# A two-layer transformer on one core: rows of scales loaded behind x, q's ones filled on GpSimd, 26 warm-up products, and the first turned maxima behind all parts

## The chip, the cores and the metric

The kernel runs on one core of a Trainium2 chip. The metric is the device time of one execution in microseconds; the median of several executions is compared. The core has five engines with a queue of instructions each: TensorE (PE, products), VectorE (DVE), ScalarE (ACT), GpSimd (POOL) and SyncE (SP, which here only issues transfers). They meet at semaphores only.

## The reference

x (1024 tokens of 256 numbers) passes through two layers; each adds attention and then a feed-forward block, both of the normalised x:

```
x = x + attn0(layernorm(x))     # 16 heads of 16; q, k, v, o with biases; ALiBi; causal
x = x + ffn0(layernorm(x))      # silu(gate) * up, then down; weights are int32 less 128, times a scale per row
x = x + attn1(layernorm(x))     # as above without biases and ALiBi
x = x + ffn1(layernorm(x))      # weights rounded to float8 e4m3, times a scale per column
```

ALiBi adds `slope[h] * (key - 1023)` to each score. A softmax needs the largest score of each query; the kernel computes it in full.

## The kernel before

**Exact products from bf16 parts.** q and k come from products in float32 (`qk` jobs 0 to 7: first q and k of heads 0 to 7 for tokens 0 to 511, jobs 0 and 1, then of heads 8 to 15, jobs 2 and 3, then the same for tokens 512 to 1023, jobs 4 to 7). Each result is split into three bf16 parts (high on ScalarE, middle on ScalarE, low on VectorE), and SyncE copies them by transfers inside the core's memory, six for each job, into `qS` and `kS`, where 96 rows (16 numbers of a head, six times) make one contraction. Below these 96 rows stand in the first layer three rows of ALiBi (in `kS`: the bias in three bf16 parts; in `qS`: ones) and two rows for the negated maximum of the query (in `kS`: ones; in `qS`: the maximum in two parts). So the score that goes into the exponential has its maximum taken off already.

**Attention** runs over 8 groups of 4 heads and 512 queries (`CGS`), in an order written out beforehand (`attention_order`): scores for the maxima (`max_scores`, L668 to L676) that VectorE reduces (L1091), a turn of a group's maxima (`turn`, L739; VectorE copies them to `mT`, L1104; SyncE sends them to `qS`, L440, `spread_max`), the scores again with the maximum taken off (`exp_scores`, L690), the exponential on ScalarE (L982), a cut along the diagonal on GpSimd (L521) and the product with v (L710). Ahead of the first exp step stand 21 score products of the first two groups and the first turn; between them TensorE does side jobs (v, the turning of the first feed-forward's weights and of the second layer's). The first exp product of a group waits for its `mT` transfer, and everything behind it on TensorE's queue waits with it. At most three score products are ahead of VectorE (three banks).

**The start.** SyncE loads x in three pieces, Wv and Wo, the tails of `kS` and `qS` (ALiBi rows and ones), then the rows of scales (`col_rows`, eight small transfers, L416 to L421) and the bias bo; ScalarE's queue loads bq, bk, Wq and Wk. TensorE runs `WARM` products of no use (L833), turns the normalised x (L616), and computes jobs 0 to 3 (L848); the second half of x is turned between jobs 1 and 2. ScalarE first puts Wq in the order by dimension (`turn_w0(0)`, L918), copies the four turned tiles out (L887), does the same for Wk and then the parts of the jobs (L910 high, L894 middle). Ahead of job 4, `turn_cols` (L828) turns the rows of scales into columns: TensorE waits there for all eight transfers, and behind it for Wv and Wo. The first feed-forward's weights are converted on GpSimd with these scales (L545).

**SyncE's order** behind the loads is a loop over the eight jobs (`spread`, L434), with the loads of other weights ahead of jobs 2 and 4, and the first group's maxima at `FIRST_MAX_BEFORE`, ahead of job 6:

```
for k in range(N_QK):
    ...
    if k == FIRST_MAX_BEFORE:
        spread_max(L, 0)
    spread(L, k)
for cg in range(1, N_CG):
    spread_max(L, cg)
```

Of the kernel before, what the change touches and what calls it, by code (L numbers as in the profile page):

```python
# [26 lines left out]
P = 128  # L27
T, C = 1024, 256
NH, HD = 16, 16
HID0, HID1 = 704, 768  # L30
NT = T // P
CH = 512
# [14 lines left out]
N_COLS = COL_S1 + 2 * HT  # L47
ZERO_POINT = 128.0
SCALE = float(HD) ** -0.5

F32, BF16, FP16, I32 = mybir.dt.float32, mybir.dt.bfloat16, mybir.dt.float16, mybir.dt.int32
ALU = mybir.AluOpType
# [6 lines left out]
QK_ROWS = len(Q_PARTS) * HD  # L59

ALIBI_ROWS = (3, 0)
MAX_ROWS = 2
X_PIECES = (slice(0, 2), slice(2, TPC), slice(TPC, NT))
TAIL_GAP = 32
K_MAX = [QK_ROWS + a for a in ALIBI_ROWS]
K_EXP = [k + MAX_ROWS for k in K_MAX]


def qk_job(n):

    return n // 2 % CJ, n // (2 * CJ), n % 2


N_QK = CJ * NC * 2
# [69 lines left out]
TURN_AHEAD = 5  # L144
FIRST_HALF_AFTER = 5
QK_FIRST = 2
WARM = 60
COLS_BEFORE = 4
V_FIRST = (5, 2)
FIRST_TURN_AHEAD = 7  # L150
FFN0_AFTER = 2
W1_AFTER = 4
FIRST_MAX_BEFORE = 6
PV_LAG = 1
W8_DOWN_AT = 3

# [82 lines left out]
def alibi_tail():  # L239

    bf16 = mybir.dt.np(BF16)
    start = 2.0 ** -0.5
    slopes = np.array([start * start ** i for i in range(NH)], np.float32)
    bias = slopes[:, None] * (np.arange(T, dtype=np.float32) - np.float32(T - 1))[None, :]
    rest = bias.astype(np.float32) / np.float32(SCALE)
    rows = []
    for _ in range(3):
        part = rest.astype(bf16)
        rows.append(part)
        rest = rest - part.astype(np.float32)  # L250
    rows += [np.ones((NH, T), bf16)] * (MAX_ROWS + ALIBI_ROWS[0])
    apart = np.zeros((len(rows), NH * NC, CH + TAIL_GAP), bf16)
    apart[:, :, 0:CH] = np.stack(rows).reshape(len(rows), NH * NC, CH)
    return apart


def two_layer_kernel(nc, a, out, tail):
    with ExitStack() as ctx:
        def sb(name, shape, dt):
            return ctx.enter_context(nc.sbuf_tensor(name, shape, dt))  # L260

        def sem(name):
            return ctx.enter_context(nc.semaphore(name))
# [11 lines left out]
        v1 = sb("v1", [P, NT, NH, 2 * HD], F32)  # L275
# [8 lines left out]
        w0 = sb("w0", [P, 4, CJ, C], F32)  # L284
# [47 lines left out]
        mask_q = sb("mask_q", [P, P], BF16)  # L332
        mask_k = sb("mask_k", [P, P], BF16)
        q_flat = qS[:, :, :, :].rearrange("p c h t -> p (c h t)")
        q_chunks = q_flat.rearrange("p (n t) -> p n t", t=CH)
        k_chunks = kS[:, :, :].rearrange("p h t -> p (h t)").rearrange("p (n t) -> p n t", t=CH)
        fT = q_flat.bitcast(F32)[:, 0:HT * T].rearrange("p (k t) -> p k t", k=HT)

# [9 lines left out]
        w0_in, wvo_in = [sem(f"w0_in{m}") for m in range(2)], sem("wvo_in")  # L348
# [7 lines left out]
        tail_in = sem("tail_in")  # L356
# [2 lines left out]
        s_full, s_free = sem("s_full"), sem("s_free")  # L359
        m_full, m_free = sem("m_full"), sem("m_free")  # L360
        tri_done = sem("tri_done")
        ones_v = sem("ones_v")
        pv_done, o_taken = sem("pv_done"), sem("o_taken")
        consts, consts_step = sem("consts"), sem("consts_step")
        stats_done, rstd_done, xn_done = sem("stats_done"), sem("rstd_done"), sem("xn_done")
# [37 lines left out]
        @block.sync  # L403
        def _(sp):
            xin = a["L0_attn_x"].rearrange("o (t p) c -> p (o t) c", p=P)
            for piece, tiles in zip(x_in, X_PIECES):
                sp.dma_start(x[:, tiles, :], xin[:, tiles, :]).then_inc(piece, 16)
            for m, n in ((2, "Wv"), (3, "Wo")):
                sp.dma_start(w0[:, m], a[f"L0_attn_{n}"].rearrange("(j p) o -> p j o", p=P)).then_inc(wvo_in, 16)
            full = HID0 // P  # L410
            sp.dma_start(k_chunks[QK_ROWS:K_EXP[0]], tail[0:ALIBI_ROWS[0] + MAX_ROWS, :, 0:CH]).then_inc(tail_in, 16)
            sp.dma_start(q_chunks[QK_ROWS:K_MAX[0]], tail[ALIBI_ROWS[0] + MAX_ROWS:, :, 0:CH]).then_inc(tail_in, 16)
            sp.wait_ge(rows_zero, 1)
            for m, n in enumerate(("gate", "up")):
                s, row = a[f"L0_ffn_s_{n}"], COL_S0 + m * HT
                sp.dma_start(col_rows[row:row + full], s[0:full * P].rearrange("(k p) -> k p", p=P)).then_inc(rows_in, 16)  # L416
                sp.dma_start(col_rows[row + full:row + HT, 0:HID0 - full * P], s[full * P:HID0].unsqueeze(0)).then_inc(rows_in, 16)
            for row, n in ((COL_SD0, "L0_ffn_s_down"), (COL_BV, "L0_attn_bv"),
                           (COL_S1, "L1_ffn_gate_scale"), (COL_S1 + HT, "L1_ffn_up_scale")):
                whole = a[n].rearrange("(k p) -> k p", p=P)  # L420
                sp.dma_start(col_rows[row:row + whole.shape[0]], whole).then_inc(rows_in, 16)  # L421
            sp.dma_start(bo[:], a["L0_attn_bo"].unsqueeze(0).to_broadcast([P, C])).then_inc(bo_in, 16)

            def spread(L, k):

                mt, c, w = qk_job(k)
                heads = slice(mt * NH // CJ, (mt + 1) * NH // CJ)
                for part, done in enumerate((hi_done, mid_done, lo_done)):
                    sp.wait_ge(done, L * N_QK + k + 1)
                    for r, stands in enumerate((Q_PARTS, K_PARTS)[w]):  # L430
                        if stands == part:
                            rows = slice(r, QK_ROWS, len(Q_PARTS))
                            dst = qS[rows, c, heads, :] if w == 0 else kS[rows, heads, c * CH:(c + 1) * CH]
                            sp.dma_start(dst, part_slots[k][:, part]).then_inc(stacked[k], 16)  # L434

            def spread_max(L, cg):

                g, c = CGS[cg]
                sp.wait_ge(mT_done, L * N_CG + cg + 1)
                sp.dma_start(qS[K_MAX[L]:K_EXP[L], c, g * G:(g + 1) * G, :], mT[:, cg % 2, :]).then_inc(m_stacked[cg % 2], 16)  # L440

            for L in range(LAYERS):
                for k in range(N_QK):
                    if (L, k) == (0, FFN0_AFTER):
                        for m, n in enumerate(("gate", "up")):
                            w = a[f"L0_ffn_wq_{n}"]
                            sp.dma_start(g0[:, m, 0:full].bitcast(I32), w[0:full * P].rearrange("(k p) i -> p k i", p=P)).then_inc(ffn0_in, 16)
                            sp.dma_start(g0[0:HID0 - full * P, m, full].bitcast(I32), w[full * P:HID0]).then_inc(ffn0_in, 16)
                    if (L, k) == (0, W1_AFTER):
                        sp.dma_start(d0[:, :, :].bitcast(I32), a["L0_ffn_wq_down"].rearrange("(j p) i -> p j i", p=P)).then_inc(ffn0d_in, 16)  # L450
                        for m, n in enumerate(("Wq", "Wk", "Wv", "Wo")):
                            sp.dma_start(w1r[:, m], a[f"L1_attn_{n}"].rearrange("(j p) i -> p j i", p=P)).then_inc(w1_in, 16)
                    if k == FIRST_MAX_BEFORE:
                        spread_max(L, 0)
                    spread(L, k)
                for cg in range(1, N_CG):
                    spread_max(L, cg)
                if L == 0:
                    sp.wait_ge(pv_done, N_STEP)
                    sp.dma_start(k_chunks[K_MAX[1]:K_EXP[1]], tail[ALIBI_ROWS[0]:ALIBI_ROWS[0] + MAX_ROWS, :, 0:CH]).then_inc(ones_k, 16)  # L460
            yout = out.rearrange("o (t p) c -> p (o t) c", p=P)
            for t in range(NT):
                sp.wait_ge(x_final, t + 1)
                sp.dma_start(yout[:, t, :], x[:, t, :]).then_inc(stored, 16)
            sp.wait_ge(stored, 16 * NT)
# [3 lines left out]
        def _(pool):  # L469
            k = [0]  # L470
# [11 lines left out]
            for m in (ident, identb):  # L482
# [3 lines left out]
                                    pattern=[[-1, P]], channel_multiplier=1)  # L486
            nc.gpsimd.affine_select(out=mask_k[:], in_=mask_k[:], compare_op=ALU.is_ge, fill=NEG, base=0,
                                    pattern=[[1, P]], channel_multiplier=-1).then_inc(consts, 1)

            nc.gpsimd.memset(v1[:, :, :, HD:2 * HD], 1.0).then_inc(ones_v, 1)  # L490

            def round_columns(w, top, dst, cols):

# [39 lines left out]
            rstd_of(0)  # L533
            rstd_of(1)
            pool.wait_ge(rstd_done, 4)

            pool.wait_ge(ffn0_in, 16 * 4)
            pool.wait_ge(a_free, A_AT[("cols",)] + 1)
# [52 lines left out]
        def _(pe):  # L591
# [228 lines left out]
            def turn_bqk():  # L820
                bank = take_a(("bqk_cols",))
                pe.wait_ge(bqk_turned, 1)
                nc.tensor.transpose(bank[:, 0:2 * CJ], bqk_dims, ident[0:2 * CJ, 0:2 * CJ]).then_inc(a_full, 1)
# [7 lines left out]
            turn_bqk()  # L831
            for _n in range(WARM):
                nc.tensor.matmul(ps[:, 7, 0:P], identb[:], mask_q[:], start=True, stop=True)  # L833
            for L in range(LAYERS):
# [26 lines left out]
                    side_job(L, side)  # L861
                if L == 0:
                    pe.wait_ge(ones_v, 1)
                    pe.wait_ge(tail_in, 16 * 2)
                else:
                    pe.wait_ge(ones_k, 16)
                attention(L)
# [5 lines left out]
        def _(act):  # L873
# [52 lines left out]
            for L in range(LAYERS):  # L926
# [44 lines left out]
                for s in range(N_STEP):  # L971
# [7 lines left out]
                    for pair in range(G // 2):  # L979
                        m = 2 * n + pair  # L980
                        act.wait_ge(s_full, m + 1)
                        nc.scalar.activation(prob[:, n % 3, 2 * pair:2 * pair + 2, off:CH],  # L982
                                             ps[:, 2 * (m % 2):2 * (m % 2) + 2, off:CH], ACT.Exp, scale=SCALE).then_inc(s_free, 1)
                    if s >= PV_LAG:
# [275 lines left out]
```

## Time and profile before

| | us |
|---|---|
| median of three runs | 449.64 |
| the three runs | 448.88, 452.99, 449.64 |
| the profiled execution | 453.61 |
| its span, first to last instruction | 451.9 |

| engine | busy us | share of the span |
|---|---|---|
| TensorE | 419.5 | 93% |
| VectorE | 301.8 | 67% |
| ScalarE | 235.9 | 52% |
| GpSimd | 161.0 | 36% |

The mean granted clock of TensorE was 0.984 of full. Busy shares are means over stages that have different limits; the change touches only the first 70 us, so those are read by themselves. Times in the rows below are microseconds from the start of the span.

### The profile page before, as it was taken

Reading aid. Unit: us, or ns where it says so; the run is one execution under the profiler, and the core shown is the slowest. Engines: PE = TensorE matmul, PEld = TensorE weight load, DVE = VectorE, ACT = ScalarE, POOL = GpSimd, SP = SyncE. Lnnn points to the kernel's source line nnn. Section 1 sums busy time; section 2 is a strip of 40 time slices with the busy share of each in tenths; the row PEclk is TensorE's granted clock in tenths of the full one; section 3 lists DMA queues with packets and bytes.
Section 4 is the critical chain, followed back from the end, with each engine's and each line's share of the span. In section 5 each row is a group of like instructions: output and inputs, shape, how many; then the busy total and the mean of one; then the engine's idle time right before and its main releaser. Section 6 shows DMA issues by size and latency. Waiting matters only on the chain.

```text
span 451.9 us, 14543 instructions
## 1 busy us (share of the span) xinstructions
PE 419.5 (93%) x6326; PEld 237.9 (53%) x6326; DVE 301.8 (67%) x609; ACT 235.9 (52%) x383; POOL 161.0 (36%) x242
## 2 busy tenths in 40 slices
PE   5799989999999979999999998998999999798997
PEld 5356654455555347434467455644545553374476
DVE  4635699999996129322234577999999971197883
ACT  3534546677687862211100552455776778724950
POOL 4108323202202222295961000235362463220780
PEclk9979999999999999999999999999999999998999
DMA  7899450000000000202000468500000000000002
GB/s 201 136 246 268 95 141 4 4 3 4 4 3 5 3 7 0 71 1 70 1 0 0 109 181 209 137 4 4 3 4 4 4 5 2 2 1 0 2 23 71
DMA packets 21657, 22.97 MB, mean 51 GB/s; under 512 B 2588, under 2 KB 20858, under 8 KB 21594
## 3 DMA queue, kind: packets, MB, share of 16 engines
q1 hardware_dynamic: 20498, 19.03, 17.4%
q0 software_dynamic: 544, 2.49, 1.9%
q8 instruction: 50, 0.82, 0.8%
q10 hardware_dynamic: 552, 0.53, 0.4%
q14 instruction: 13, 0.11, 0.1%
HBM read 8.27 MB, written 1.05 MB: 21 GB/s over the span
## 4 chain that ended last, share of the span: by engine, by line
PE 69%; DVE 17%; ACT 5%; DMA 3%; issue 2%; SPq 2%; POOL 1%; ACTq 0%; DVEq 0%
DVE mx L1091 11%; PE ps L710 10%; PE ps L690 10%; PE ps L668 10%; PE ps L793 9%; PE ps L808 5%; PE ps L848 5%; PE ps L798 5%; ACT prob L982 4%; PE ps L607 4%; PE ps L816 3%; DMA col_rows<-in_L_ffn_up_scale 3%; PE ps L676 1%; DVE stats L1055 1%; DVE xn L1164 1%
## 5 line engine op out<-in xcount | busy, mean ns | idle before, releaser
L1091 DVE TENSOR_REDUCE mx<-ps 128x1 f32<-128x512 f32 (+3 forms) x304 | 182.2, 656 | 24.5 <-PE ps L676 21.9
L982 ACT ACTIVATE prob<-ps 128x1024 f32<-128x1024 f32 (+1 forms) x192 | 145.5, 812 | 70.1 <-PE ps L690 69.5
L668 PE MATMUL ps<-kS,qS 99*32 99x512 bf16 (+21 forms) x1536 | 113.7, 320 | 4.8 <-DVE mx L1091 2.9
L521 POOL TENSOR_SCALAR_AFFINE_SELECT prob<-prob 128x256 f32<-128x256 f32 x128 | 51.9, 412 | 159.5 <-ACT prob L982 158.2
L690 PE MATMUL ps<-qS,kS 101*32 101x512 bf16 (+7 forms) x1536 | 96.3, 327 | 3.8 <-ACT prob L982 3.5
L710 PE MATMUL ps<-prob,v 128*32 128x512 f32 (+3 forms) x768 | 80.2, 489 | 2.1 <-POOL prob L521 1.4
L668 PEld LDWEIGHTS ps<-kS,qS 99*32 99x32 bf16 (+1 forms) x1536 | 43.5, 95 | 53.5 <-DVE mx L1091 30.1
L690 PEld LDWEIGHTS ps<-qS,kS 101*32 101x32 bf16 (+1 forms) x1536 | 35.4, 96 | 32.5 <-ACT prob L982 16.8
L673 PE MATMUL ps<-mask_q,identb 128*32 128x32 bf16 (+1 forms) x1024 | 51.6, 185 | 0.0
L676 PE MATMUL ps<-mask_q,identb 128*32 128x96 bf16 (+1 forms) x512 | 45.9, 197 | 0.0
L793 PE MATMUL ps<-xnT,gu0T 128*128 128x512 f32 (+1 forms) x96 | 42.2, 596 | 0.7 <-ACT xnT L887 0.7
L673 PEld LDWEIGHTS ps<-mask_q,identb 128*32 128x32 bf16 x1024 | 28.5, 97 | 10.9 <-issue 6.2
L676 PEld LDWEIGHTS ps<-mask_q,identb 128*32 128x32 bf16 x512 | 28.8, 98 | 5.4
L793 PEld LDWEIGHTS ps<-xnT,gu0T 128*128 128x128 f32 (+1 forms) x96 | 17.0, 181 | 24.5 <-issue 23.5
L1162 DVE RECIPROCAL rec<-ps 128x16 f32<-128x16 f32 x16 | 3.8, 236 | 35.5 <-PE ps L760 35.5
L1204 DVE TENSOR_TENSOR qS<-ps,rest 128x512 f32<-128x512 f32 (+1 forms) x12 | 8.3, 690 | 28.3 <-PE ps L793 28.3
L710 PEld LDWEIGHTS ps<-prob,v 128*32 128x32 f32 x768 | 19.5, 109 | 12.2 <-POOL prob L521 7.2
L1028 ACT ACTIVATE rest<-ps 128x512 f32<-128x512 f32 (+1 forms) x12 | 7.2, 596 | 32.2 <-PE ps L793 32.2
L808 PE MATMUL ps<-d0T,qS 128*128 128x256 f32 (+1 forms) x96 | 23.9, 396 | 0.0
L798 PE MATMUL ps<-xnT,gu 128*128 128x512 f16 x96 | 22.2, 393 | 1.6 <-DVE xnT L1178 1.6
L887 ACT COPY xnT<-ps 128x256 f32<-128x256 f32 x24 | 7.2, 385 | 29.8 <-PE ps L616 29.8
L587 POOL TENSOR_TENSOR kS<-prob,qS 128x512 bf16<-128x512 f32 x12 | 18.1, 1520 | 11.4 <-ACT qS L1013 11.1
(135 smaller groups left out, 528.4 us busy)
## 6 DMA issues: line engine op xcount, KB each, us to landing
qS<-parts SPq DMA_DIRECT2D x24, 128.0 KB, 3.4
kS<-parts SPq DMA_DIRECT2D x24, 128.0 KB, 3.7
qS<-prob SPq DMA_DIRECT2D x12, 128.0 KB, 6.9
kS<-prob SPq DMA_DIRECT2D x12, 128.0 KB, 6.4
qS<-xn SPq DMA_DIRECT2D x12, 128.0 KB
kS<-xn SPq DMA_DIRECT2D x12, 128.0 KB
out<-x SPq DMA_DIRECT2D x8, 128.0 KB, 1.7
oT<-in_L_ffn_gate_w POOLq DMA_DIRECT2D x1, 768.0 KB, 5.0
```

Of the source, the lines that this page charges most:

```text
L521: nc.gpsimd.affine_select(out=square, in_=square, compare_op=ALU.is_ge, fill=0.0, base=0, pattern=[[0, 2], [1, P]], channel_multiplier=-1) ...
L668: mmi = nc.tensor.matmul(span[r:r + STRIP, 0:seen], qS[0:K_MAX[L], c, g * G + h, qt * P + r:qt * P + r + STRIP], kS[0:K_MAX[L], g * G + h, ...
L673: mmi = nc.tensor.matmul(span[r:r + STRIP, keys - P + r:keys - P + edge], identb[:, r:r + STRIP], mask_q[:, r:edge], start=False, stop=True)
L676: mmi = nc.tensor.matmul(span[r:r + STRIP, keys - P + r + STRIP:keys], identb[:, r:r + STRIP], mask_q[:, r + STRIP:P], start=True, stop=True)
L690: mmi = nc.tensor.matmul(bank[r:r + STRIP, off:CH], kS[0:K_EXP[L], h, kt * P + r:kt * P + r + STRIP], qS[0:K_EXP[L], c, h, off:CH], start= ...
L710: mmi = nc.tensor.matmul(bank[32 * h:32 * h + 32, off:CH], v1[:, kt, g * G + h, :], prob[:, n % 3, h, off:CH], start=kt == 0, stop=s == LA ...
L793: mmi = nc.tensor.matmul(bank[0:r, :], gu0T[:, m, j, ht * P:ht * P + r], xnT[:, j, c * CH:(c + 1) * CH], start=j == 0, stop=j == CJ - 1)
L798: mmi = nc.tensor.matmul(bank[:, :], gu1[:, m, j, ht * P:(ht + 1) * P], xhl[:, j, s, c * CH:(c + 1) * CH], start=j + s == 0, stop=j == CJ ...
L808: mmi = nc.tensor.matmul(bank[:, 0:C], fT[0:r, ht, t * P:(t + 1) * P], d0T[0:r, ht, :], start=ht == 0, stop=ht == HT - 1)
L848: mmi = nc.tensor.matmul(bank[:, :], attn_w(L, w)[:, j, mt * P:(mt + 1) * P], xnT[:, j, c * CH:(c + 1) * CH], start=j == 0, stop=j == CJ - 1)
L982: nc.scalar.activation(prob[:, n % 3, 2 * pair:2 * pair + 2, off:CH], ps[:, 2 * (m % 2):2 * (m % 2) + 2, off:CH], ACT.Exp, scale=SCALE).th ...
L1091: ins = nc.vector.tensor_reduce(mx[:, slot, qt, heads[0]:heads[-1] + 1, part], src, AX_X, ALU.max)
```

## The change

It does five things. The eight transfers of the rows of scales are issued right behind x, ahead of Wv, Wo and the tail of `kS`. The ones below q are not loaded but filled on GpSimd, as 32-bit words that hold two bf16 ones, behind the last rstd of the first normalisation; the fill of v's ones moves there too, and TensorE waits for the new semaphore `ones_q` ahead of attention. The warm-up products are 26 in place of 60. In the first layer the first group's maxima are sent after job 7, in the second layer ahead of job 6 as before.

```diff
+TWO_ONES = float(np.array([0x3F803F80], np.uint32).view(np.float32)[0])
...
-WARM = 60
+WARM = 26
...
-FIRST_MAX_BEFORE = 6
+FIRST_MAX_BEFORE = (N_QK, 6)
...
-    rows += [np.ones((NH, T), bf16)] * (MAX_ROWS + ALIBI_ROWS[0])
+    rows += [np.ones((NH, T), bf16)] * MAX_ROWS
...
-            for m, n in ((2, "Wv"), (3, "Wo")):
-                sp.dma_start(w0[:, m], a[f"L0_attn_{n}"].rearrange("(j p) o -> p j o", p=P)).then_inc(wvo_in, 16)
             full = HID0 // P
-            sp.dma_start(k_chunks[QK_ROWS:K_EXP[0]], tail[0:ALIBI_ROWS[0] + MAX_ROWS, :, 0:CH]).then_inc(tail_in, 16)
-            sp.dma_start(q_chunks[QK_ROWS:K_MAX[0]], tail[ALIBI_ROWS[0] + MAX_ROWS:, :, 0:CH]).then_inc(tail_in, 16)
             sp.wait_ge(rows_zero, 1)
...
                 sp.dma_start(col_rows[row:row + whole.shape[0]], whole).then_inc(rows_in, 16)
+            for m, n in ((2, "Wv"), (3, "Wo")):
+                sp.dma_start(w0[:, m], a[f"L0_attn_{n}"].rearrange("(j p) o -> p j o", p=P)).then_inc(wvo_in, 16)
+            sp.dma_start(k_chunks[QK_ROWS:K_EXP[0]], tail[:, :, 0:CH]).then_inc(tail_in, 16)
             sp.dma_start(bo[:], a["L0_attn_bo"].unsqueeze(0).to_broadcast([P, C])).then_inc(bo_in, 16)
...
-                for k in range(N_QK):
+                for k in range(N_QK + 1):
...
-                    if k == FIRST_MAX_BEFORE:
+                    if k == FIRST_MAX_BEFORE[L]:
                         spread_max(L, 0)
-                    spread(L, k)
+                    if k < N_QK:
+                        spread(L, k)
...
-            nc.gpsimd.memset(v1[:, :, :, HD:2 * HD], 1.0).then_inc(ones_v, 1)
-
...
             pool.wait_ge(rstd_done, 4)
+            nc.gpsimd.memset(v1[:, :, :, HD:2 * HD], 1.0).then_inc(ones_v, 1)
+            pool.wait_ge(ones_v, 1)
+            nc.gpsimd.memset(q_flat[QK_ROWS:K_MAX[0]].bitcast(F32), TWO_ONES).then_inc(ones_q, 1)
+            pool.wait_ge(ones_q, 1)
...
                     pe.wait_ge(ones_v, 1)
-                    pe.wait_ge(tail_in, 16 * 2)
+                    pe.wait_ge(tail_in, 16)
+                    pe.wait_ge(ones_q, 1)
```

## Rows read from the trace of the kernel before

**Rows 1.** Chain that ended last, 0 to 60: start, length, what.

```profile
8.65 13.06 DMA col_rows<-in_L_ffn_up_scale
```

**Rows 2.** Timeline of TensorE, 17 to 62: start, length, engine, line; in brackets idle time before.

```profile
21.84 0.27 PE L828 MATMUL ps<-ident,col_rows 28*128 28x28 f32 x1 [2.72 <-DMA col_rows<-in_L_ffn_up_scale]
22.05 3.78 PE L848 MATMUL ps<-xnT,gu 128*128 128x512 f32 x4
...
30.24 1.88 PE L848 MATMUL ps<-xnT,gu 128*128 128x512 f32 x4
```

**Rows 3.** Busy times by half microseconds, both layers; granted clock third from the end.

```profile
21.00:21.50 0.50, 0.00 (x0) 0.00 (x0) 0.50 (x2) 0.00 (x0) 0.00 (x0) 0.66 1.18 246
...
27.50:28.00 0.50, 0.50 (x2) 0.17 (x1) 0.49 (x1) 0.00 (x0) 0.00 (x0) 0.52 1.14 350
...
280.50:281.00 0.50, 0.30 (x9) 0.24 (x13) 0.30 (x1) 0.00 (x0) 0.00 (x0) 0.57 0.93 197
```

**Rows 4.** Timeline of SyncE's queue, 0 to 70; groups of six are one job's q or k.

```profile
5.61 1.03 SPq L416 DMA_DIRECT2D col_rows<-in_L_ffn_s_gate  x1
...
13.91 3.99 SPq L434 DMA_DIRECT2D qS<-parts  x6
...
40.35 3.83 SPq L434 DMA_DIRECT2D kS<-prob  x6
54.27 0.70 SPq L440 DMA_DIRECT2D qS<-mT  x1
55.02 4.80 SPq L434 DMA_DIRECT2D qS<-xn  x6
59.86 4.70 SPq L434 DMA_DIRECT2D kS<-xn  x6
64.61 4.90 SPq L440 DMA_DIRECT2D qS<-mT  x2
```

**Rows 5.** Timeline of all engines, 0 to 14 (L848 cut off at 14).

```profile
4.69 4.85 PE L833 MATMUL ps<-mask_q,identb 128*128 128x128 bf16 x60
...
7.06 1.16 ACT L918 COPY gu<-w 128x256 f32<-128x256 f32 x2 [2.11 <-DMA w<-in_L_attn_Wq]
...
9.80 1.20 ACT L887 COPY xnT<-ps 128x256 f32<-128x256 f32 x4 [1.58 <-PE ps L616]
...
11.14 3.24 PE L848 MATMUL ps<-xnT,gu 128*128 128x512 f32 x7 [0.73 <-ACT xnT L887]
...
11.22 1.15 ACT L918 COPY gu<-w 128x256 f32<-128x256 f32 x2 [0.23 <-DMA w<-in_L_attn_Wk]
```

**Rows 6.** Timeline of GpSimd, 0 to 45.

```profile
2.68 1.80 POOL L490 MEMSET v<- 128x2048 f32 x1
...
33.02 7.01 POOL L545 TENSOR_SCALAR prob<-prob,cols 128x256 f32<-128x256 int32 x12 [19.65 <-DMA prob<-in_L_ffn_wq_up]
```

**Rows 7.** Timelines of TensorE and VectorE, start of attention in both layers.

```profile
57.46 0.39 PE L690 MATMUL ps<-qS,kS 101*32 101x512 bf16 x4
...
67.40 0.62 PE L690 MATMUL ps<-qS,kS 101*32 101x512 bf16 x8
...
68.85 13.91 DVE L1091 TENSOR_REDUCE mx<-ps 128x1 f32<-128x512 f32 x24
...
283.33 0.64 PE L690 MATMUL ps<-qS,kS 98*32 98x512 bf16 x3
...
294.89 5.47 DVE L1091 TENSOR_REDUCE mx<-ps 128x1 f32<-128x512 f32 x9
```

**Rows 8.** Busy times by two microseconds: PE, PEld, DVE, ACT, POOL, clock, DMA share, GB/s.

```profile
48.00:50.00 2.00, 2.00 (x69) 1.65 (x70) 1.30 (x3) 1.06 (x2) 1.26 (x2) 1.00 0.64 145
...
58.00:60.00 2.00, 1.85 (x82) 1.22 (x74) 1.93 (x6) 1.82 (x2) 0.41 (x1) 1.00 0.59 158
```

More of the change, by code:

```diff
@@ L334, in two_layer_kernel @@
         q_flat = qS[:, :, :, :].rearrange("p c h t -> p (c h t)")
-        q_chunks = q_flat.rearrange("p (n t) -> p n t", t=CH)
         k_chunks = kS[:, :, :].rearrange("p h t -> p (h t)").rearrange("p (n t) -> p n t", t=CH)
@@ L361, in two_layer_kernel @@
         tri_done = sem("tri_done")
-        ones_v = sem("ones_v")
+        ones_v, ones_q = sem("ones_v"), sem("ones_q")
         pv_done, o_taken = sem("pv_done"), sem("o_taken")
```

## The prediction

> **What bounds the kernel now.** I read the first 70 us of four views: what TensorE waits for, the clock it is granted, SyncE's queue in order of time, and the start of attention. The rest of the program is the same in both kernels, so only the moment at which it is entered can move.
>
> TensorE stands still once before attention: for 2.72 us, until 21.84, it waits for the rows of scales [rows 2]. The last of these eight transfers was issued at 8.65 and took 13.06 us to land [rows 1]. The wait costs a second time: the granted clock fell to half at about 21.2 and came back at about 28.0 [rows 3], and the first projection behind the wait took 3.78 us where a later one took 1.88 [rows 2]. So the late rows cost TensorE 2.7 us of standing and at least 1.9 us of slow work.
>
> The second view is SyncE's queue [rows 4]. From 13.91 it issues without a pause worth the name until the last part of projection 5 is out at 40.35 + 3.83 = 44.18: six transfers take about 3.84 us, 0.64 each. Then it waits for the first group's turned maxima (mT), issues them at 54.27, and only then the twelve transfers of projections 6 and 7, in 4.80 and 4.70 us. The exp stage starts at 57.46 [rows 7], 3.2 us after the issue of mT. So in the kernel before, SyncE has ten idle microseconds ahead of mT, and mT sets when the exp stage starts.
>
> The third view is what the exp stage leads into. From 68.85 VectorE reduces 24 maxima in 13.91 us with no gap [rows 7]; it is the bound there. Whatever moves the start of the exp stage (call it E, 57.46) moves the end of the kernel nearly one for one.
>
> **The change part by part.**
>
> *Fewer warm-up products (60 to 26).* They run from 4.69 to about 9.4, and the four drains of the transposed x begin on ScalarE at 9.80, after an idle time of 1.58 us that ended with TensorE's transposes [rows 5]. With 34 products fewer TensorE is free at about 7.3, and ScalarE is free at 7.06 + 1.16 = 8.22, when its copies of Wq end. The drains then start at 8.22, 1.58 us earlier, and projection 0 starts at about 9.6 in place of 11.14. The second copy pair (Wk) waited for its transfer until 11.22 [rows 5]. If Wk lands no earlier, the copy ends at 12.37, and projection 1, which began half way through the 3.7 us of both, near 13.0, gains 0.6. Wk may land earlier because Wv and Wo no longer stand behind x: they are issued some 3.4 us later. SyncE's queue hangs on both projections, by their high and middle parts. So its busy stretch begins 0.6 to 1.58 us earlier; I take 1.1, the middle, as nothing in the rows prefers an end.
>
> *Rows right behind x.* The eight issues stand before Wv and Wo; they begin at about 2.3 in place of 5.61 [rows 4] and no longer behind the two tails. I expect them to land by 12. The wait of 2.72 us goes, and with it the fall of the clock: TensorE's lead is 2.7 + 1.9 = 4.6 us at least (the other products of the slow stretch add to it), and 1.1 from the first part: some 5.7 to 6.3 us. TensorE would be ready for the exp stage at 57.46 - 6 = 51.5. What is late next is in the last part below. Wv and Wo are issued later by the eight issues, and are wanted at about 18; bo and the k tail are wanted at 31 and later. A late Wo would cost TensorE what the rows cost now, but out of a lead that, as is seen below, is not used.
>
> *q's ones on GpSimd.* One transfer of 96 KB leaves SyncE's queue, in a stretch where SyncE then waits for projection 0 anyway: nothing is gained. On GpSimd the fill of v took 1.80 us for 2048 elements a partition [rows 6]. q's rows have 16 x 2 x 512 bf16, which is 8192 elements of 4 bytes: 4 times as many, 7.2 us if it goes by length. Both fills now stand behind the last rstd. GpSimd was idle there for 19.65 us up to 33.02 [rows 6], that is from 13.4; two fills end at 13.4 + 1.8 + 7.2 = 22.4, about 8 us before attention wants them and ahead of the weights it converts next, which even moved earlier by 1.6 us are there at 31.4. Cost nothing; without that cover it would be 9 us. In the worst case (a fill of three partitions twice as dear by element) it ends at 29.6, still in time.
>
> *First mT behind all parts.* This is the part that decides. Before, mT stood before projections 6 and 7; now the twelve transfers go first. With everything 1.1 us earlier, SyncE is done with projection 5 at 44.18 - 1.1 = 43.1. mT would be turned at about 48, but SyncE now issues projections 6 and 7 first: 4.80 + 4.70 + 0.04 = 9.54 us, to 52.6. Then mT: 52.65, and 3.2 us to the exp stage: E = 55.9, against 57.46, a gain of 1.6. The bounds of this term: -1.1 with the Wk copy not earlier, -2.1 with the full 1.58; and if the twelve issues took 3.83 each six, like those of projection 5, another 1.84 less, -3.9. Parts 6 and 7 themselves are wanted by the sixth group, long after, so their being earlier brings nothing.
>
> So TensorE, ready at 51.5, stands idle for about 4.4 us, and VectorE with it, since the products behind the first exp product in TensorE's order are not issued. Two costs come with this. First, VectorE has no backlog at E. The second layer shows that state: there it was through its maxima when the exp stage began at 283.33, and the 24 maxima began at 294.89, 11.56 later, against 11.39 in the first layer [rows 7]. Cost 0.2. Second, the clock. Before, 2.7 us of idleness brought it down, and in the second layer a looser stretch did so at 280.5 [rows 3]. The low stretch lasted 6.8 us in the first case, 6.1 us of them with TensorE at work. An idle time of 4.4 us should bring it down by 53.6, so TensorE begins the exp stage at half clock, for 0 to 6.1 us. In the stretch 58 to 60, TensorE was busy 1.85 of 2 us and VectorE 1.93 [rows 8]; at half clock such work takes TensorE up to 1.85 times as long, a loss of up to 0.46 us in each slow us, 2.8 in all. The ends of products are modelled, so busy 1.85 is more than what binds. I take 1.3, from the bounds 0 and 2.8.
>
> *Sum:* -1.6 + 0.2 + 1.3 = -0.1 us. The profiled execution took 453.61 us, of which 451.9 are its span; it becomes 453.5. The median of the three timed runs is 449.64, 0.9% below the profiled one. On the median: 449.5. Bounds: -3.9 + 0.2 + 0 = -3.7, and -1.1 + 0.2 + 2.8 = +1.9.
>
> **A rule weighed against the rows.** mT is issued right behind twelve transfers that may still be under way. The turned maxima of the second group were in just that place before: issued at 64.61, behind the last part of projection 7 [rows 4], and the exp product that waits for them ran at 67.40 [rows 7], so they landed within 2.8 us. For this reason I keep 3.2. The Trainium skill (DMA: Bandwidth & Descriptors, section "Queues, rings and completion order") speaks against that: a transfer's increment of the semaphore lands only after all earlier writes of the same DMA engine, over all of its queues. By this rule mT inherits every backlog; the rows of scales behind the tails are what it would look like, while the trace's mT at 64.61 shows no such delay. It is the second rival.
>
> **The rivals.**
> 1. *The clock is not up for the first projections* (slower than before). The 60 products took 4.85 us, 0.081 each [rows 5], between what the two clock levels give for 128 columns (0.107 at 1.2 GHz and 0.053 at 2.4), so an estimated 31 of them were slow, until about 8. The 26 would end just before that, and then TensorE has little to do until 9.6. If it then runs projections 0 and 1 at half clock, they take 3.7 us each: projection 1 ends near 17 in place of 14.8, and SyncE's stretch starts 2.1 later than before in place of 1.1 earlier. E = 57.4 + 2.2, the sum is +2.1 + 0.2 + 1.3 = +3.6: 453.2. It decides when projection 1 ends later than 14.8. For it: those first products are nearly all the work TensorE gets. Against: transposes and projections follow within 1.5 us, and the fall came only after some 2 us of full idleness. Chance 0.12.
> 2. *mT lands late behind the parts.* The DMA engines were still at work 4 us after SyncE's last issue at 44 (share 0.64 in 48 to 50 [rows 8]). Projections 6 and 7 themselves load them only to 0.59 [rows 8], so a backlog of 4.3 us shrinks by 0.4 x 9.5 = 3.8 before mT comes. If it does not shrink: +4.3, in all +4.2: 453.8. By the skill's rule above it is this case. Chance 0.08.
> 3. *No clock cost, and cheap issues:* -3.7: 445.9. Chance 0.12.
> 4. *The rows or Wo land late all the same,* the change not doing what it says. TensorE loses its lead, but E is set by SyncE, and there is no idle time to lower the clock: -1.6 + 0.2 = -1.4: 448.2. Chance 0.10.
> 5. *TensorE's lead comes through,* because the queue's order costs less than I read: -6: 443.6. Chance 0.05. Against it stand 48 issues of 0.64 us in one queue.
>
> **How the numbers follow.** The forecast itself has 0.53. Its time is 449.5. The range takes in rivals 1, 3, 4 and the unknown terms: 445.7 to 453.8; outside are rival 5, part of 2, and tails. Some 1% (4.5 us) is what a measurement of this kernel can tell from no change: its three runs lie 0.9% apart. Below 445.1 fall rival 5 and about half of rival 3, 0.11; above 454.1 half of rivals 1 and 2, 0.10; the rest, 0.79, is within 1%.
>
> **What the changed kernel's profile would show.** Right, if: no wait of TensorE for the rows and full clock from 12 to 50; the stretch of part transfers on SyncE's queue begins near 12.8 and runs with no gap through projection 7 to about 52.6, mT directly behind; TensorE idle for some 4 us before the first exp product near 56; half clock for a few us behind it; the 24 maxima beginning near 69. Wrong, if mT is issued much before 52, if SyncE's queue has a gap before projection 6, if projection 1 ends after 14.8, or if mT takes more than 4 us to land.

## The result and the profile after

The changed kernel takes 458.7 us in the median (457.18 to 459.31, four runs) against 450.72 for the kernel before: the ratio is 1.0189, 95% interval 1.0152 to 1.0226. The profiled execution took 459.03 us with a span of 457.3. The forecast was "no change", 449.5, at most 453.8; the kernel is 8 us slower. Here and below a few executions lie more than 1.5% above the fastest of their kernel: the medians include them, the ratios leave them out.

VectorE and GpSimd, the timeline of all engines of the changed kernel from 9 to 30 us:

```profile
12.65 8.99 DVE L1069 TENSOR_SCALAR xn<-x,mv,rstd 128x256 f32<-128x256 f32 x2 [0.32 <-POOL rstd L529]
12.67 1.80 POOL L534 MEMSET v<- 128x2048 f32 x1
14.54 6.95 POOL L536 MEMSET qS<- 3x8192 f32 x1
21.56 1.39 DVE L1147 SCALAR_TENSOR_TENSOR rest<-ps,bqk,parts 128x512 f32<-128x512 f32 x2
22.33 1.28 ACT L897 CAST parts<-rest 128x512 bf16<-128x512 f32 x2 [8.19 <-DVE rest L1147]
```

Two writes of xn, which take 0.73 us together when nothing is beside them, last 8.99 us: the first is done when the first fill on GpSimd ends (12.67 + 1.80 = 14.47), the second when the second fill ends (14.54 + 6.95 = 21.49). The chain that ended last has the second of them as a piece of its own:

```profile
14.55 7.10 DVE xn L1069
```

Most of the loss follows from this. SyncE's queue of the changed kernel, 0 to 80 us:

```profile
2.33 0.45 SPq L412 DMA_DIRECT2D col_rows<-in_L_ffn_s_gate  x1
...
12.51 12.30 SPq L433 DMA_DIRECT2D qS<-parts  x6
24.85 3.83 SPq L433 DMA_DIRECT2D kS<-parts  x6
...
50.12 5.00 SPq L433 DMA_DIRECT2D qS<-xn  x6
55.16 5.08 SPq L433 DMA_DIRECT2D kS<-xn  x6
60.30 16.04 SPq L439 DMA_DIRECT2D qS<-mT  x3
```

The first six part transfers take 12.30 us where they took 3.99 [rows 4]: the high part is issued at 12.51, 1.4 us earlier than before, but the middle part waits on ScalarE for `rest`, which stands behind xn on VectorE. From there the queue runs with no gap, and mT comes last, at 60.30 in place of 54.27. TensorE, same kernel, 0 to 62 us (the last line from 60 to 65):

```profile
4.67 2.95 PE L835 MATMUL ps<-mask_q,identb 128*128 128x128 bf16 x26
...
9.74 3.67 PE L850 MATMUL ps<-xnT,gu 128*128 128x512 f32 x8 [0.56 <-ACT xnT L890]
...
21.79 0.66 PE L618 MATMUL ps<-ident,xn 128*128 128x128 f32 x2 [6.60 <-DVE xn L1069]
22.24 5.44 PE L850 MATMUL ps<-xnT,gu 128*128 128x512 f32 x8
27.61 0.24 PE L830 MATMUL ps<-ident,col_rows 28*128 28x28 f32 x1
...
62.45 0.40 PE L692 MATMUL ps<-qS,kS 101*32 101x512 bf16 x4 [2.24 <-DMA qS<-mT]
```

The wait for the rows of scales is gone (27.61 has no idle time before it), and in its place stands one of 6.60 us for xn. Jobs 2 and 3 behind it begin at half clock, which lasts until about 26, and take 5.44 us for what takes 3.60. The exp stage (E, its first product) starts at 62.45, against 57.46 [rows 7], after 2.24 us of waiting for mT. It starts at full clock; the clock falls about 1 us later, at 63.5, and stays at half until about 70.2. The windows of two microseconds, granted clock third from the end:

```profile
22.00:24.00 2.00, 2.00 (x5) 0.97 (x5) 1.64 (x3) 1.64 (x4) 0.00 (x0) 0.50 0.00 0
...
62.00:64.00 2.00, 1.55 (x62) 1.04 (x66) 0.45 (x1) 0.83 (x1) 0.00 (x0) 0.87 0.03 8
64.00:66.00 2.00, 1.87 (x35) 1.01 (x27) 1.93 (x5) 1.22 (x2) 0.82 (x2) 0.50 0.00 0
```

The 24 maxima behind E, where VectorE is the bound, begin at 75.74, 13.29 us after E; in the kernel before they began 11.39 us after it [rows 7].

```profile
75.74 13.90 DVE L1094 TENSOR_REDUCE mx<-ps 128x1 f32<-128x512 f32 x24
```

### The profile page after: what moved, and what is told of

The parts are those of the page before. It is cut to its first block, busy times and chain, and to the rows that moved or that the text cites. A ratio compares the mean times of both kernels' runs of the same rounds, so it can differ in the third digit from the quotient of the medians.

```text
span 457.3 us, 14476 instructions
## 1 busy us (share of the span) xinstructions
PE 418.5 (92%) x6292; PEld 236.8 (52%) x6292; DVE 310.0 (68%) x609; ACT 236.3 (52%) x383; POOL 167.8 (37%) x243
## 4 chain that ended last, share of the span: by engine, by line
PE 67%; DVE 17%; ACT 6%; SPq 5%; issue 2%; POOL 1%; DMA 1%; ACTq 0%; DVEq 0%
PE ps L712 11%; PE ps L692 11%; DVE mx L1094 10%; PE ps L795 9%; PE ps L670 8%; PE ps L850 6%; PE ps L810 5%; PE ps L800 5%; SPq L433 5%; ACT prob L985 4%; PE ps L818 3%; PE ps L609 2%; DVE xn L1069 2%; PE ps L678 1%; DVE stats L1058 1%
## 5 line engine op out<-in xcount | busy, mean ns | idle before, releaser
L670 PE MATMUL ps<-kS,qS 99*32 99x512 bf16 (+20 forms) x1536 | 114.3, 323 | 5.0 <-DVE mx L1094 3.3
L692 PE MATMUL ps<-qS,kS 101*32 101x512 bf16 (+7 forms) x1536 | 97.7, 331 | 6.0 <-ACT prob L985 3.6
L678 PE MATMUL ps<-mask_q,identb 128*32 128x64 bf16 (+1 forms) x512 | 45.8, 198 | 0.0
L675 PEld LDWEIGHTS ps<-mask_q,identb 128*32 128x32 bf16 x1024 | 29.4, 99 | 11.9 <-issue 7.0
L678 PEld LDWEIGHTS ps<-mask_q,identb 128*32 128x32 bf16 x512 | 29.0, 99 | 5.5 <-issue 0.5
L800 PE MATMUL ps<-xnT,gu 128*128 128x512 f16 x96 | 21.0, 379 | 1.6 <-DVE xnT L1181 1.6
```

The lines of the kernel that those rows point to most:

```text
L670: mmi = nc.tensor.matmul(span[r:r + STRIP, 0:seen], qS[0:K_MAX[L], c, g * G + h, qt * P + r:qt * P + r + STRIP], kS[0:K_MAX[L], g * G + h, ...
L675: mmi = nc.tensor.matmul(span[r:r + STRIP, keys - P + r:keys - P + edge], identb[:, r:r + STRIP], mask_q[:, r:edge], start=False, stop=True)
L678: mmi = nc.tensor.matmul(span[r:r + STRIP, keys - P + r + STRIP:keys], identb[:, r:r + STRIP], mask_q[:, r + STRIP:P], start=True, stop=True)
L692: mmi = nc.tensor.matmul(bank[r:r + STRIP, off:CH], kS[0:K_EXP[L], h, kt * P + r:kt * P + r + STRIP], qS[0:K_EXP[L], c, h, off:CH], start= ...
L800: mmi = nc.tensor.matmul(bank[:, :], gu1[:, m, j, ht * P:(ht + 1) * P], xhl[:, j, s, c * CH:(c + 1) * CH], start=j + s == 0, stop=j == CJ ...
```

## The experiments

Each kernel was compared with runs of the kernel before on the same chip; the ratio's 95% interval stands in brackets. E is read from the profiled execution of each.

### The fills later

The changed kernel with one line, so that both fills come behind VectorE's last xn:

```diff
             rstd_of(1)
             pool.wait_ge(rstd_done, 4)
+            pool.wait_ge(xn_done, NT)
             nc.gpsimd.memset(v1[:, :, :, HD:2 * HD], 1.0).then_inc(ones_v, 1)
             pool.wait_ge(ones_v, 1)
             nc.gpsimd.memset(q_flat[QK_ROWS:K_MAX[0]].bitcast(F32), TWO_ONES).then_inc(ones_q, 1)
```

> The changed kernel, with both fills on GpSimd behind VectorE's last write of the normalised x (xn_done at 8) in place of behind the last rstd. Theory P (the fill of q's ones holds VectorE's second xn write for 7.1 us, and with it the low part of projection 0 and SyncE's queue): the write at 12.65 takes 0.73 us for two again, the first six part transfers no 12.3 us but about 4, mT is issued near 52, the first exp product runs near 54.5 in place of 62.45: some 8 us less than the changed kernel, 450 to 451. Theory Q (the place of mT in SyncE's queue is the cause, the fill's stall is cover): within 2 us of the changed kernel, 457 to 459. Theory W (26 warm-up products are too few, the clock is the cause): the same 457 to 459.

Measured: 452.14 us against 450.03, ratio 1.0041 [1.0007, 1.0074]. Of the 1.9% loss 0.4% is left: the fills at that place cost 6 to 7 us. Both fills still run beside VectorE here (12.90 to 21.68), but beside instructions with two tensor inputs, which take what they take elsewhere (0.75 and 0.68 us). Lines of the profile (SyncE, TensorE, and the two-microsecond windows):

```profile
51.47 17.07 SPq L439 DMA_DIRECT2D qS<-mT  x3
...
54.02 0.62 PE L693 MATMUL ps<-qS,kS 101*32 101x512 bf16 x4 [4.21 <-DMA qS<-mT]
...
56.00:58.00 2.00, 2.00 (x39) 1.58 (x31) 1.72 (x5) 1.27 (x2) 0.61 (x2) 0.50 0.00 0
58.00:60.00 2.00, 1.69 (x30) 0.99 (x32) 1.91 (x4) 0.00 (x0) 0.21 (x1) 0.50 0.00 0
```

This is close to the picture that the prediction drew for the whole change: SyncE's queue without a gap, mT at 51.5, TensorE idle for 4.21 us, half clock from about 52.1 to 62.3. So the term that the prediction had at nothing was most of the loss. Its queue and its fall of the clock are there; their sizes are compared below.

### mT ahead of job 6 again

```diff
-FIRST_MAX_BEFORE = (N_QK, 6)
+FIRST_MAX_BEFORE = (6, 6)
```

> The changed kernel, with the first mT ahead of job 6 again in the first layer too; the fills stay where they stall VectorE. Theory P: SyncE is through job 5 at 50.1, mT is turned at 56.8 and issued at once in place of 60.3, the first exp product runs near 59.3, 3 us earlier, and the clock stays up for another 1 to 1.5: 454 to 455. Theory Q: the whole loss comes back, 450 to 451. Theory W: 457 to 459 less what Q gives, no change of the clock in the first 30 us.

Measured: 456.37 us, ratio 1.0144 [1.0102, 1.0187]; E = 60.22, 2.2 us earlier than in the changed kernel, with no wait for mT. The order alone does not bring the loss back; theory Q, taken as the cause of all, falls, and as a smaller second cause it stands: E shows it, while the times alone (1.0144 and 1.0189, with intervals that overlap) would not.

### Both edits

> The changed kernel with both edits: fills behind VectorE's last xn write, mT ahead of job 6. Theory P with the prediction's reading of the queue: TensorE's lead comes through, mT is turned near 48 and issued at once, the first exp product runs near 51.5 against 57.46 in the kernel before: 444 to 446. Theory Q alone: as the run with mT ahead of job 6. Rival: SyncE's later transfers of jobs 6 and 7 delay the second group's mT, so that part of the lead is lost: 447 to 449.

Measured: 446.43 us against 450.03, ratio 0.9915 [0.9877, 0.9953], ten runs from 444.43 to 450.49. This version is 0.9% faster than the kernel before, a small difference, but the interval does not reach 1. Its profiled execution was the slowest of the ten and shows the first rival of the prediction at work: jobs 0 and 1 take 6.73 us in place of 3.67, as if at half clock for most of that time (job 4 at half clock took 3.78 where later ones took 1.88 [rows 2]). The clock column of the profile reads 1.00 there, as it does over the slow warm-up products; near the start only the durations show the slow level.

```profile
10.82 6.73 PE L851 MATMUL ps<-xnT,gu 128*128 128x512 f32 x8 [1.47 <-ACT xnT L891]
```

With that, E = 53.97 and 450.49 us. The two edits together give 12.3 us over the changed kernel (by medians), more than the late fills alone (6.6) and the order alone (2.3) together. The moments at which TensorE had nothing left but the wait for mT say why: 60.21 in the changed kernel (62.45 - 2.24), 49.81 with late fills (54.02 - 4.21). The stall cost TensorE 10.4 us, of which the late mT hid 2; with the fills late, the order costs the 4.2 us of waiting.

### The kernel before with only the fills of the change

The memsets behind the last rstd, `ones_q`, and the q tail no longer loaded; all else as before.

> The kernel before with only the fills of the change (both behind the last rstd, q's ones no longer loaded); rows of scales, 60 warm-up products and mT ahead of job 6 as before. Theory P: one VectorE write of xn takes over 7 us, jobs 2 and 3 start near 23.5, SyncE's queue and the first exp product come 6 to 7 us later: 456 to 458. Theories Q and W: no change, 449 to 452.

Measured: 455.16 us, ratio 1.0145 [1.0086, 1.0204], with the same 8.99 us for two writes of xn and E = 59.22. One part of the change done alone makes most of the loss, with mT issued as soon as it is turned (56.03) and no wait for it. It is 0.8 us under the range that theory P gave.

### What holds VectorE: one instruction, or shared turns

The changed kernel with q's fill cut into eight instructions at the same place:

```diff
-            nc.gpsimd.memset(q_flat[QK_ROWS:K_MAX[0]].bitcast(F32), TWO_ONES).then_inc(ones_q, 1)
+            q_words = q_flat[QK_ROWS:K_MAX[0]].bitcast(F32)
+            for n in range(8):
+                ins = nc.gpsimd.memset(q_words[:, n * 1024:(n + 1) * 1024], TWO_ONES)
+            ins.then_inc(ones_q, 1)
```

> The changed kernel, with the fill of q's ones cut into 8 instructions of 1024 elements, at the same place. Theory P1 (VectorE's instruction waits for the end of the one GpSimd instruction that is under way): the second xn write waits 0.9 us or a little more in place of 7.1, the first 1.5 as before; jobs 2 and 3 start near 15 to 16; 451 to 453. Theory P2 (both engines share a port by turns of data, so that VectorE is slow as long as fills go on): the write is still 5 to 9 us long; 457 to 459.

Timeline of all engines, 9 to 22:

```profile
12.06 3.02 DVE L1072 TENSOR_SCALAR xn<-x,mv,rstd 128x256 f32<-128x256 f32 x2 [0.32 <-POOL rstd L529]
12.09 1.80 POOL L534 MEMSET v<- 128x2048 f32 x1
13.95 7.38 POOL L538 MEMSET qS<- 3x1024 f32 x8
```

Measured: 454.07 us, ratio 1.0069 [1.0036, 1.0102]. The two writes take 3.02 us: the first is done at the end of the fill of v (12.09 + 1.80 = 13.89) and the second at the end of the first piece (about 0.92 us each), while the other pieces run on to 21.3 beside VectorE's next work. So VectorE waits for the end of one GpSimd instruction and no longer (P1). The median lies above the 451 to 453 that P1 gave, and above that with late fills. That would fit the 2.3 us that are left of the stall (3.02 less 0.73), and E = 56.50 in this profile against 54.02; the intervals of the two ratios overlap.

### What holds VectorE: the form of its own instruction

The changed kernel, long fill in place, but the four writes in question take rstd as a second tensor input:

```diff
+                    if (ln, half) == (0, 1):
+                        nc.vector.scalar_tensor_tensor(xn[:, t], x[:, t], mv[:, t, 0:1], rstd[:, t:t + 1].to_broadcast([P, C]),
+                                                       ALU.subtract, ALU.mult).then_inc(xn_done, 1)
+                        continue
                     nc.vector.tensor_scalar(xn[:, t], x[:, t], mv[:, t, 0:1], rstd[:, t:t + 1],
                                             ALU.subtract, ALU.mult).then_inc(xn_done, 1)
```

> The changed kernel with its long fill where it is, but the four last writes of the first normalised x made with another VectorE instruction: rstd as a second tensor input (broadcast) in place of a column operand; the result is the same sum and product. Theory P3 (it is the form of VectorE's instruction that wants what GpSimd holds): no stall, the four writes take about 0.5 us each beside the fill; 451 to 453. Theory P4 (any VectorE instruction that reads and writes this memory stands while GpSimd fills): the stall stays, 457 to 459.

Timeline of all engines, 9 to 22:

```profile
12.44 0.88 DVE L1070 SCALAR_TENSOR_TENSOR xn<-x,mv,rstd 128x256 f32<-128x256 f32 x2 [0.21 <-POOL rstd L529]
12.47 1.80 POOL L534 MEMSET v<- 128x2048 f32 x1
14.33 6.92 POOL L536 MEMSET qS<- 3x8192 f32 x1
```

Measured: 452.1 us, ratio 1.0043 [1.0013, 1.0073], the same as with late fills, and E = 54.03, again the same. The same subtraction and product, beside the same fill, take 0.88 us for two where they took 8.99; undisturbed they are 0.15 us dearer than the old form. So it is the old form that needs what a fill on GpSimd holds (P3).

By the Trainium skill ("SBUF — State Buffer", section "Who interferes with whom") VectorE in a two-port mode, which a `tensor_scalar` can enter, and GpSimd exclude each other for a whole instruction, and an instruction with two inputs from SBUF is not held by a GpSimd instruction that only writes. These two runs agree with both halves of it: 8.99 us against 3.02 in pieces, and against 0.88 with two inputs. That the old form ran in such a mode is an inference from the page; the runs show only that its form decides.

### The rows of scales alone

The kernel before, with only the loads reordered: the rows behind x, then Wv, Wo, both tails, bo.

> The kernel before with only the loads reordered: rows of scales right behind x, then Wv, Wo, both tails, bo. Fills on GpSimd, 60 warm-up products and mT ahead of job 6 as before. By the prediction's reading: no wait of TensorE at 19 to 22, full clock there, a lead of 4.6 us or more; mT is issued when it is turned, since SyncE has idle time there; the first exp product near 52 to 53, 445 to 447. Rival (SyncE's later transfers take the lead away, or Wo lands late): 449 to 451.

Measured: 449.1 us against 449.93, ratio 0.9976 [0.9946, 1.0006]: at best a small gain, not the 3 to 5 us expected; the time is the rival's, its two reasons are not seen in the profile. The mechanism is there: in the profiled execution (447.05, the fastest of ten) the wait is gone (TensorE at 19.09 with no idle time) and E = 51.40, where SyncE issues mT at 48.21, as soon as it is turned:

```profile
48.21 0.70 SPq L440 DMA_DIRECT2D qS<-mT  x1
...
51.40 0.39 PE L690 MATMUL ps<-qS,kS 101*32 101x512 bf16 x4
```

What is wrong is what it was held against, as the next run shows.

### The kernel before once more

> The kernel before, unchanged, for a second profile. Theory: the profiled execution of before (453.61) was an unusual one, and a usual one near 450 shows TensorE waiting for the rows with no fall of the clock behind it, jobs 4 to 7 at full clock, and the first exp product near 54 in place of 57.46. Rival: the wait and the fall are the same, and the 3.6 us lie elsewhere.

Measured: 450.27 us. Timelines of TensorE and SyncE:

```profile
4.67 6.03 PE L833 MATMUL ps<-mask_q,identb 128*128 128x128 bf16 x60
...
21.95 0.21 PE L828 MATMUL ps<-ident,col_rows 28*128 28x28 f32 x1 [1.67 <-DMA col_rows<-in_L_ffn_up_scale]
22.09 1.99 PE L848 MATMUL ps<-xnT,gu 128*128 128x512 f32 x4
...
51.11 0.70 SPq L440 DMA_DIRECT2D qS<-mT  x1
...
54.30 0.39 PE L690 MATMUL ps<-qS,kS 101*32 101x512 bf16 x4
```

Against rows 2 and 4 of the first profile: the 60 products take 6.03 us, not 4.85, since more of them were slow (about 0.11 us each until near 10, where in the first profile it was until near 7.5), and so the wait for the rows is 1.67, not 2.72; no fall of the clock follows it, job 4 takes 1.99 us, not 3.78; and E = 54.30, not 57.46. The profiled execution on which the prediction rests had the fall for 6.8 us and a mean clock of 0.984, and it belongs with the slowest: 28 runs of the kernel before beside these last experiments span 447.56 to 455.63, with a mean clock of 0.991 or 0.992 in the fourteen fastest, as in this second profile, 0.988 or 0.989 in the next eleven, and 0.984 or 0.985 in the three slowest. The mean does not say where in the kernel the clock was low, so how often it falls at this place is not known. In the profile with the order alone, whose start is that of the kernel before, the wait was 0.61 us and job 4 took 1.98. Where the clock does not fall, the rows have only these 0.6 to 1.7 us to give. Of the 2.9 us by which E is earlier with the rows moved (51.40 against 54.30), 1.1 come from warm-up products that took 4.89 us in that execution, not 6.03.

The two profiles also show what releases the exp stage of the kernel before. TensorE has no idle time ahead of its first exp product, at 57.46 [rows 7] or at 54.30, and no instruction waits for this mT. The chain of the first profile does not pass through mT either; around E it goes from TensorE's score products to VectorE's reducing:

```profile
55.72 0.24 PE ps L668 x3
55.98 0.08 PE ps L676
56.09 3.29 DVE mx L1091 x6
```

From the issue of mT to the exp product it is 3.11 to 3.19 us in all nine profiles with mT ahead of job 6, and in none of them does TensorE wait for it. This is the work that TensorE still has to do behind the turn, not the time of the transfer.

### 26 warm-up products alone

> The kernel before with 26 warm-up products in place of 60 and nothing else. By the prediction's reading TensorE's 1.6 us at the start are lost again at the wait for the rows of scales (until 21.84 in the profile of before), which a longer idle time there makes likelier to bring the clock down: no change, or up to 3 us slower, 450 to 453. Rival (the start counts by itself): 1 to 1.5 us faster, 448.5 to 449.

Measured: 452.39 us against 450.97, ratio 1.0034 [1.0000, 1.0067]; the wait for the rows grew to 3.87 us and job 4 behind it took 3.55. A shorter start ahead of a wait gives nothing. It probably lets the clock fall more often: none of the ten executions has a mean clock above 0.989, where half of those of the kernel before have 0.991 or 0.992.

### mT behind job 7 alone

> The kernel before with only the first mT of the first layer moved behind job 7. SyncE would be through job 7 at 44.2 + 9.6 = 53.8. If the first exp product of a usual execution comes at 57.5 as in the profile of before, mT loses nothing: 449.5 to 450.5. If it comes near 54 (usual executions of the kernel before have no fall of the clock at the rows, since their median is 3.6 us under the profiled one), mT is late by 3 us: 452.5 to 454, and more with a fall of the clock.

Timelines of SyncE and TensorE:

```profile
52.23 17.64 SPq L440 DMA_DIRECT2D qS<-mT  x3
...
57.20 0.49 PE L691 MATMUL ps<-qS,kS 101*32 101x512 bf16 x4 [2.35 <-DMA qS<-mT]
```

Measured: 454.68 us against 450.97, ratio 1.0099 [1.0067, 1.0131]. VectorE had mT ready at 50.7, SyncE issued it at 52.23, and here it took 5 us from there to the exp product, not 3.2, with TensorE waiting. The DMA engines were still at work on what stood ahead; the share of their time is the last number but one, behind the clock, in windows of two microseconds:

```profile
54.00:56.00 2.00, 0.36 (x13) 0.23 (x13) 1.34 (x3) 0.00 (x0) 0.00 (x0) 1.00 0.93 196
56.00:58.00 2.00, 0.80 (x13) 0.48 (x17) 0.00 (x0) 0.00 (x0) 0.00 (x0) 0.84 0.17 55
```

The same holds for every profile with mT behind job 7: from its issue to the exp product 2.15 us (the changed kernel), 2.55 (late fills), 3.18 (fill in pieces), 2.06 (two inputs) and 4.97 here, and each time the DMA share of the half microsecond ahead of E has come down to about 0.2 or less. E is 2.9 us later than in the second profile of before. So the new order costs 1% by itself, just above the 452.5 to 454 expected; by SyncE's times alone, against the first profile (mT turned at 54.2), it would have been free.

### 60 and 36 warm-up products in the faster version

Both edits (late fills, mT ahead of job 6), with `WARM = 60` and `WARM = 36`:

> The changed kernel with late fills and mT ahead of job 6 (as the run a3_both), and 60 warm-up products in place of 26. Theory C (26 products end at the edge of the clock's rise, so that some executions compute jobs 0 and 1 at half clock, 6.7 us in place of 3.7): with 60 no execution does so, the highest of the runs comes down from 450.5 to under 448, and the median lies at 445 to 446, though the good executions start jobs 0 and 1 1.5 us later. Rival (the spread comes from elsewhere, and the 1.5 us count): the same spread, 444.4 to 450.5, moved up by 1 to 1.5 us, median 447.5 to 448.

> The version with late fills and mT ahead of job 6, with 36 warm-up products, which end near 8.1 where ScalarE is through with Wq (8.2). Theory C (26 products end at the edge of the clock's rise): the start keeps the 1.5 us that 60 products cost, and no execution computes jobs 0 and 1 at half clock: median 445.5 to 446.5, highest under 448.5. Rival: the spread of a3_both stays (444.4 to 450.5), as the rise depends on more than the number of products.

Measured: with 60, 448.55 us, ratio 0.9957 [0.9933, 0.9981], twelve runs within 446.97 to 449.14; with 36, 447.9 us, ratio 0.9932 [0.9897, 0.9967], 445.32 to 450.02. With 60 the spread is down from 6.1 to 2.2 us, as theory C has it (though the highest is 449.1, not under 448), and the median is up by about 2, as the rival has it and more (it gave 448 at most). With 36 the spread, 4.7 us, stays near that of 26, the rival again; the median is 1.4 us above the range of theory C. Its profiled execution had jobs 0 and 1 at full clock and E = 50.13, and yet took 447.9, with the clock at half from about 273.5 to 277.5, 386 to 390 and 403 to 407. So products at the start are not the only source of the spread; where the rest comes from is open. Between 26 and 36 these runs don't decide.

## Why the prediction was wrong

**The step that failed** is "q's ones on GpSimd": "Cost nothing", with GpSimd's idle 19.65 us as the cover [rows 6]. The length was right, 7.2 us forecast and 6.95 measured; the cover was read on the wrong engine. The idle time of GpSimd was free, but VectorE's last xn writes stand in its first microsecond, and in that form they cannot run while a fill runs. Put in place of the nothing, the term is 62.45 - 54.02 = 8.4 us of E (the changed kernel against the one with late fills), and 6.6 us of the median. That single change takes the measured time to 452.14, inside the range.

**What releases the exp stage** was misread too. "mT sets when the exp stage starts" is not so in the kernel before: TensorE's own products and VectorE's reducing do, and mT has slack. The 3.2 us "to land" were TensorE's work. So a later mT could at best be free, and it cost as soon as TensorE was ready before it.

**"Fewer warm-up products"**: right in the size of the lead. Jobs 0 and 1 began at 9.74 (forecast about 9.6), SyncE's first part at 12.51 (forecast near 12.8). The risk that 26 end too early (rival 1) is real: it appeared in one of the profiles, 6.73 us for the two jobs in place of 3.67. That rival's price has a slip: with the forecast's own term (1.6 gained for a start 1.1 earlier) a start 2.1 later gives +1.6, not +2.1, and +3.1 in all.

**"Rows right behind x"**: right that the wait goes; wrong in what it is worth. The forecast let TensorE gain 4.6 us at least, with the fall of the clock in it; the second profile of the kernel before has a wait of 1.67 us and no fall, and rows moved alone gave 0.2%. I had divided the profiled time by the median and noted 0.9%, but did not ask what the profiled execution had that the others lacked.

**"First mT behind all parts"**: SyncE's queue came out as described, with mis-sized terms. The forecast had E = 55.9 without the fills' stall; measured 54.02, as SyncE was through job 7 at 51.4, not 52.6, and the exp product followed 2.55 us behind mT's issue, not 3.2. But the E to compare with is nearer 54.30 than 57.46, so the gain of 1.6 us was 0.3. The idle time (4.4 forecast, 4.21 measured) fits by luck in part: both its ends were 1.7 to 1.9 us early. The half clock behind it came, for some 8 us with TensorE at work, where the forecast had 6.1 at most. Together with the missing backlog it cost 13.91 - 11.39 = 2.5 us between E and the 24 maxima (67.93 with late fills), where 0.2 + 1.3 stood in the sum, within its bounds. With both terms as measured the sum is -0.3 + 2.5 = +2.2 us, and the median with late fills lies 2.1 above that of the kernel before. Alone, this part costs 1.0%.

**The rivals**: none of the five held the cause. Rival 2, the late landing, is refuted for the changed kernel: mT was issued at 60.30 right behind twelve part transfers and the exp product ran at 62.45, 2.2 us later. With the order alone it took 4.97 us, with TensorE waiting and the DMA engines busy, as the rival has it; in the four other profiles with this order 2.06 to 3.18. What sets it within these bounds was not tested. Rival 5 does not come true: TensorE's lead comes through only with the old order (E = 50.13 with 36 warm-up products, and 49.81 is when TensorE would have been ready with late fills).

**The direction**: E moved from 54.30 to 62.45, by 8.15 us, and the 24 maxima from 65.69 to 75.74, by 10.05. The two profiled executions differ by 8.76 us and the medians by 8.0. That the last is so near to the 8.15 is partly luck: from E to the end of the execution the profiles take between 395.3 and 399.7 us, with stretches of half clock at other places each time. Two profiles of one kernel, 57.46 with 453.61 and 54.30 with 450.27, show the nearly one-for-one exchange that the prediction built on.

## What to carry to other kernels

An engine's idle time is a cover only for work that takes nothing from the others: before moving a long fill onto GpSimd, look at what VectorE writes in the same stretch and in which form, and put the fill behind it or cut it in pieces. When one transfer can release the next stage, look first whether anything waits for it now: no idle time ahead of the stage means that it has slack, not that it sets the pace. If it does release the stage, the place of its issue in a queue counts by what is queued ahead of it, and by what the DMA engines still carry, at the moment when it is ready, and that must be worked out for the kernel that all the other edits leave. When the profiled execution is not near the median, ask first what is special in it, since a fall of the clock in it may be counted as a gain that other executions can't give.

## What the runs showed of the hardware

A fill of 3 partitions x 8192 words on GpSimd takes 6.95 us, one of 128 x 2048 takes 1.80: 0.85 and 0.88 ns for each element of a partition, with 3 partitions as with 128. While either runs, VectorE's `tensor_scalar` from float32 to float32 with two column operands (0.41 us alone) stands until the instruction on GpSimd ends, even where its recorded start is 0.02 us ahead of the fill's (12.65 and 12.67); a `scalar_tensor_tensor` of the same size passes (0.88 us for two). An mT transfer right behind twelve part transfers took 2.1 to 5.0 us from its issue to the product that waited for it. The warm-up's 60 products took from 4.85 to 6.03 us in two executions of one kernel. In these two, a wait of 2.72 us brought the clock down and one of 1.67 did not; in two other kernels one of 3.87 did and one of 0.61 did not.
